# Moving four products per sequence from VectorE to ScalarE, and zero products on TensorE, in a Mamba and mixture-of-experts layer

## What is computed

```python
dA = jnp.exp(dt[..., None] * A)                      # 512 channels, 16 states
dBu = (dt * xc)[..., None] * Bm[:, :, None, :]
_, h = jax.lax.associative_scan(comb, (dA, dBu), axis=1)
y = jnp.einsum('blds,bls->bld', h, Cm) + D_skip * xc
y = y * jax.nn.silu(z)
return x + y @ W_out
```

## Time and profile before

| | |
|---|---|
| three runs, median (lowest to highest) | 1532.35 us (1527.24 to 1533.11) |
| profiled execution, its own time | 1532.31 us |
| span of its instructions | 1529.8 us |
| mean granted clock of TensorE, share of full | 0.934 |
| busy: PE, PEld, DVE, ACT, POOL | 1316.2, 1065.5, 1224.3, 786.7, 1044.4 us |

### The profile page before, as it was taken

The page is one execution under the profiler, slowest core; times in us unless marked ns, Lnnn a source line. Parts: engine busy times, 40 slices in busy tenths (PEclk is TensorE's granted clock), DMA queues, the critical chain, the costliest instruction groups (busy, mean ns, idle before and its releaser), DMA issues.

```text
span 1529.8 us, 26003 instructions
## 1 busy us (share of the span) xinstructions
PE 1316.2 (86%) x8004; PEld 1065.5 (70%) x8004; DVE 1224.3 (80%) x2149; ACT 786.7 (51%) x1385; POOL 1044.4 (68%) x943
## 2 busy tenths in 40 slices
PE   8567786877877998898798799979999999999997
PEld 3345564565555766666666566768899999999997
DVE  5889999999989999999999998988465555555554
ACT  4766767767866885886887687667000000000000
POOL 2775888799989899989999988987433352222222
PEclk9778898889979999999999999999999999999999
DMA  7212121324224344244343233577967797766662
GB/s 224 97 56 63 55 56 49 97 73 88 81 71 138 115 139 124 75 142 146 106 129 122 76 115 106 183 238 219 303 191 204 217 275 203 210 196 190 200 205 76
DMA packets 129344, 216.34 MB, mean 141 GB/s; under 512 B 17948, under 2 KB 74792, under 8 KB 129080
## 3 DMA queue, kind: packets, MB, share of 16 engines
q1 hardware_dynamic: 110376, 183.86, 39.1%
q0 software_dynamic: 16064, 27.62, 7.1%
q10 hardware_dynamic: 2768, 3.21, 0.9%
HBM read 178.34 MB, written 37.22 MB: 141 GB/s over the span
## 4 chain that ended last, share of the span: by engine, by line
PE 45%; POOL 18%; DVE 16%; issue 11%; ACT 7%; DMA 2%; SPq 1%; POOLq 0%; DVEq 0%; ACTq 0%
PE psum L1719 14%; PE psum L1735 13%; POOL dBu L885 12%; DVE w_sb L2022 8%; PE psum L1526 6%; DVE y L2033 3%; PE psum L1535 2%; ACT psum L1140 2%; ACT hc L1124 2%; PE psum L1687 1%; POOL rows_d L803 1%; PE psum L1674 1%; DVE w_sb L2003 1%; PE psum L1492 1%; DVE xc L2003 1%
## 5 line engine op out<-in xcount | busy, mean ns | idle before, releaser
L885 POOL TENSOR_TENSOR dBu<-w_sb,brep 128x512 f32<-128x512 f32 x512 | 642.9, 1319 | 35.5 <-issue 14.8
L2022 DVE TENSOR_TENSOR_SCAN w_sb<-psum,dBu 128x512 f32<-128x512 f32 x512 | 611.7, 1212 | 54.3 <-ACT psum L1140 34.3
L1140 ACT ACTIVATE psum<-w_sb,aneg 128x512 f32<-128x512 f32 x512 | 350.2, 692 | 123.0 <-DVE w_sb L2022 120.1
L1526 PE MATMUL psum<-ident,w_sb 128*128 128x128 f32 x2048 | 306.2, 297 | 116.8 <-DVE y L2033 73.8
L1526 PEld LDWEIGHTS psum<-ident,w_sb 128*128 128x128 f32 x2048 | 250.1, 152 | 195.1 <-DVE y L2033 108.3
L872 POOL DMA_INDIRECT out<-dBu,token x59 | 92.2, 1563 | 296.3 <-DMA out<-dBu,token 231.8
L1124 ACT ACTIVATE hc<-psum,ct 128x512 f32<-128x512 f32 x256 | 175.0, 683 | 106.1 <-PE psum L1526 73.8
L1535 PE MATMUL psum<-ident,hc 128*128 128x128 f32 x1024 | 168.2, 295 | 35.3 <-ACT hc L1124 24.4
L1535 PEld LDWEIGHTS psum<-ident,hc 128*128 128x128 f32 x1024 | 130.3, 151 | 76.8 <-ACT hc L1124 38.4
L2033 DVE SCALAR_TENSOR_TENSOR y<-psum,ct,y 128x512 f32<-128x512 f32 x240 | 174.9, 729 | 10.7 <-PE psum L1526 9.7
L1719 PE MATMUL psum<-xn,win 128*128 128x128 f32 x928 | 110.1, 278 | 3.2 <-issue 3.2
(11 more groups left out here) (274 smaller groups left out, 1747.8 us busy)
## 6 DMA issues: line engine op xcount, KB each, us to landing
brep<-b_d SPq DMA_DIRECT2D x128, 256.0 KB, 4.0
expert_pieces<-in_W SPq DMA_DIRECT2D x30, 1024.0 KB, 5.9
win<-in_W SPq DMA_DIRECT2D x29, 1024.0 KB
expert_pieces<-in_W SPq DMA_DIRECT2D x42, 512.0 KB, 5.3
dBu<-rows_d SPq DMA_DIRECT2D x35, 257.0 KB, 2.9
w_sb<-in_W SPq DMA_DIRECT2D x8, 1024.0 KB, 10.1
xg<-rows_d SPq DMA_DIRECT2D x22, 257.0 KB, 2.8
h_d<-hmod SPq DMA_DIRECT2D x8, 512.0 KB, 4.0
```

Of the source, the lines that this page charges most:

```text
L885: nc.gpsimd.tensor_tensor(dBu[:, i % RING, :], u[p][:, c, :], brep[:, s % 4, :], ALU.mult).then_inc(s_dBu, 1)
L1140: nc.scalar.activation(dA[:, i % DA_RING, :], dt[p][:, c, :], ACT.Exp, scale=aneg[:, c, s:s + 1]).then_inc(s_dA, 1)
L1526: last = nc.tensor.transpose(T[:, i // DT, c * P:(c + 1) * P], hs[s % 2][:, c, i * P:(i + 1) * P], ident[:, :])
L2022: nc.vector.tensor_tensor_scan(hs[s % 2][:, c, :], dA[:, i % DA_RING, :], dBu[:, (n * UNITS + i) % RING, :], 0.0, ALU.mult, ALU.add).then_ ...
```

## The change

The two products of state 0 move from VectorE to ScalarE in all eight sequences (`times_c_begin`; it writes `y` itself, so VectorE's form for state 0 goes). In sequences 0 to 6 the second-tile products of states 3 and 5 also move to ScalarE (`times_c_apart`), each into a tile of its own; `y_t` adds these to tile 1 with eight more transposes. TensorE multiplies zeros three times ahead of sequence 0's states, and three times after `xf_t` in state 9 of sequences 1 to 3. In sequence 7, `out_proj` leaves out the identity products, and VectorE adds the residual (`hres`) instead, one addition per half.

```diff
+APART = (3, 5)
...
+        def states_apart(n):
+            return APART if n < NB - 1 else ()
...
+            def times_c_begin(n, p, k):
+                if k == 0:
+                    act.wait_ge(s_c, n + 1)
+                    after(act, s_base, n - 1)
+                act.wait_ge(s_tr, n * UNITS + 2 * k + 1)
+                nc.scalar.activation(y[p][:, k, :], T[:, 0, :], ACT.Copy, scale=ct[:, p, k, 0:1]).then_inc(s_y, 1)
+
+            def times_c_apart(n, p, s):
+                act.wait_ge(s_tr, n * UNITS + TI * s + 3)
+                if s == APART[0]:
+                    after(act, s_yT, n)
...
+                nc.scalar.activation(apart(s), T[:, 0, :], ACT.Copy, scale=ct[:, p, 1, s:s + 1]).then_inc(s_y, 1)
...
+                    if s == 1:
+                        times_c_begin(n, p, 0)
                     times_c_before(n, p, s, 0, has_o)
                     if has_p and s == 1:
                         norm(n + 1, (0, 1))
...
                     decays(n, p, s, (2,), has_o)
+                    if s == 1:
+                        times_c_begin(n, p, 1)
...
+                    if s - 1 in states_apart(n):
+                        times_c_apart(n, p, s - 1)
                     decays(n, p, s, (3,), has_o)
...
                 for i in range(DT):
-                    for c in range(CH):
-                        last = nc.tensor.transpose(YT[:, i, c * P:(c + 1) * P], y[n % 2][:, i, c * P:(c + 1) * P], ident[:, :])
+                    parts = [y[n % 2][:, i, :]] + [apart(s) for s in states_apart(n) if i == 1]
...
                 at = slice((i % 2) * D, (i % 2 + 1) * D)
-                nc.tensor.matmul(Q[:, OB, at], ident[:, :], hres[:, i, :], start=True, stop=False)
+                if n < NB - 1:
+                    nc.tensor.matmul(Q[:, OB, at], ident[:, :], hres[:, i, :], start=True, stop=False)
...
+                if not has_o:
+                    pe.wait_ge(s_sp0, 2)
+                    pe.wait_ge(s_relu0, CH)
+                    for i in range(3):
+                        nc.tensor.matmul(T[:, 1, :], zeros[:, :], ones[:, :].unsqueeze(1).to_broadcast([P, TI, P]), start=True, stop=True)
                 for s in range(NS):
...
                         xf_t(n - 1)
+                        if n <= 3:
+                            add_zeros(3)
...
+                if n == NB - 1:
+                    dve.wait_ge(s_hload, 16 * NB)
+                    link(nc.vector.tensor_tensor(projected, hres[:, at, :], projected, ALU.add), n)
...
-                    add_y(n, p, s, 0)
+                    if s > 0:
+                        add_y(n, p, s, 0)
...
-                    add_y(n, p, s, 1)
+                    if s > 0 and s not in states_apart(n):
+                        add_y(n, p, s, 1)
```

More of the change, by code:

```diff
@@ L133, in program @@
         hc = sb("hc", [P, 2, DIN])
+        apart_first = sb("second_tile_apart", [P, 2, DIN])
         gT = sb("gT", [P, CH, L])
@@ L338, in program, with apart @@
         BANK = (1, 0, 1, 0)
+        def states_apart(n):
+            return APART if n < NB - 1 else ()
+        def apart(s):
+            j = APART.index(s)
+            if j < 2:
+                return apart_first[:, j, :]
+            return modo[:, 2 * j - 4:2 * j - 2, :].rearrange("p m d -> p (m d)")
         XB, OB = 0, 1
@@ L1124, in times_c @@
                 nc.scalar.activation(hc[:, k, :], T[:, 1, :], ACT.Copy, scale=ct[:, p, DT + k, s:s + 1]).then_inc(s_hc, 1)
+            def times_c_begin(n, p, k):
[8 more added lines that the diff above has]
+                    after(act, s_yT, n)
+                if s > 12:
+                    after(act, s_base, n)
+                nc.scalar.activation(apart(s), T[:, 0, :], ACT.Copy, scale=ct[:, p, 1, s:s + 1]).then_inc(s_y, 1)
             def times_c_before(n, p, s, k, has_before):
@@ L1548, in y_t @@
                 for i in range(DT):
-                    for c in range(CH):
-                        last = nc.tensor.transpose(YT[:, i, c * P:(c + 1) * P], y[n % 2][:, i, c * P:(c + 1) * P], ident[:, :])
+                    parts = [y[n % 2][:, i, :]] + [apart(s) for s in states_apart(n) if i == 1]
+                    for j, part in enumerate(parts):
+                        for c in range(CH):
+                            last = nc.tensor.matmul(YT[:, i, c * P:(c + 1) * P], part[:, c * P:(c + 1) * P], ident[:, :],
+                                                    start=(j == 0 and c == 0), stop=(j == len(parts) - 1), is_transpose=True,
+                                                    skip_group_check=True)
                 last.then_inc(s_yT, 1)
@@ L1555, in out_proj @@
                     after(pe, s_xnt, projected)
-                    pe.wait_ge(s_hload, 16 * (n + 1))
+                    if n < NB - 1:
+                        pe.wait_ge(s_hload, 16 * (n + 1))
                 if i == 2:
@@ L1563, in out_proj @@
                         pe.wait_ge(s_gate, n * CH + c + 1)
-                    last = nc.tensor.matmul(Q[:, OB, at], gT[:, c, i * P:(i + 1) * P], wout[:, c, :], start=False, stop=(c == CH - 1))
+                    last = nc.tensor.matmul(Q[:, OB, at], gT[:, c, i * P:(i + 1) * P], wout[:, c, :],
+                                            start=(n == NB - 1 and c == 0), stop=(c == CH - 1))
                 last.then_inc(s_op, 1)
@@ L2027, in add_y @@
                 c_s = ct[:, p, i, s:s + 1]
-                if s == 0:
-                    after(dve, s_base, n - 1)
-                    ins = nc.vector.tensor_scalar(y[p][:, i, :], T[:, 0, :], c_s, None, ALU.mult)
-                else:
-                    dve.wait_ge(s_y, DT * (n * NS + s - 1) + i + 1)
-                    ins = nc.vector.scalar_tensor_tensor(y[p][:, i, :], T[:, 0, :], c_s, y[p][:, i, :], ALU.mult, ALU.add)
-                ins.then_inc(s_y, 1)
+                dve.wait_ge(s_y, DT * (n * NS + s - 1) + i + 1)
+                nc.vector.scalar_tensor_tensor(y[p][:, i, :], T[:, 0, :], c_s, y[p][:, i, :], ALU.mult, ALU.add).then_inc(s_y, 1)
             def o_skip(n, p):
```

## The result

The changed kernel takes 1541.29 us (median of 11 runs, 1538.81 to 1554.24), the kernel before 1531.83 in as many: a ratio of 1.0069, interval 1.0051 to 1.0087. It is slower by more than the 0.5% that a measurement can tell. The forecast was 1531.0. The profiled execution took 1540.64 us, with a span of 1538.8.

The account below looks back on a forecast made before the run. VectorE was taken as nearly full in the recurrence, with ScalarE's room varying by state, and TensorE as the epilogue's bound. 4.75 - 8.3 + 3.8 - 1.7 = -1.45 us from 1532.31 gave 1530.9, rounded to 1531; range 1514 to 1541.

Parts of the forecast that it names:

- the zeros of state 9: TensorE's three zero products in sequences 1 to 3: 3.8 us lost in sum, bounds 3.2 won and 9 lost.
- the 8.3 us of states 3 and 5: Second-tile products moved to ScalarE: 13 x 0.64 = 8.3 us won, as ScalarE's idle time fits them.
- 1.0 won in sequence 1: Zeros just ahead of 10.2 us at clock 0.50: up to 3.2 us back if lifted, less 1.8 own cost.
- the working: The prediction's own sum over the changed places, apart from its rivals: -1.45 us, so 1531 us.
- 9 lost: The losing bound on the zeros' term, against 3.2 us won at the other end.
- The walk: States 3 and 5: ScalarE's product fits before its next decay, the fourth scan still finds it; 0.64 us won each.
- State 0, 4.75 us lost: Products moved to ScalarE, which has no room: later fourth decay, extra y transposes; 0.2 + 0.6 + 1.95 + 2.0 us lost.
- The projection, 1.7 us won: Epilogue: four identity products of 0.43 us leave a TensorE that never pauses; VectorE's additions hide in idle time.
- The first: Rival: VectorE bounds everywhere, all 30 products give 0.64 us each, zeros hidden; 1511.4 us, chance 0.20.
- The third: Rival: zeros keep TensorE at 2.4 GHz through sequence 1's stage and cost nothing; 1523.9 us, chance 0.10.
- The second, the other side: Rival: dt projection after state 9; zeros cost fully, late tiles halve states 3 and 5's win; 1539.3 to 1543, chance 0.13.
- late tiles: The second rival's reason for losing half of states 3 and 5's win, leaving 4.15 us won.

## Why the prediction was wrong

Two steps of the sum failed: the zeros of state 9, whose term left out the low clock behind them, and the 8.3 us of states 3 and 5. In the profiled executions, after less before, the 9.0 us of the span come from these places (the roundings add 0.1):

| place | forecast | measured |
|---|---|---|
| states 0 to 3, all sequences | +4.75 | +2.7 |
| states 4 to 7, all sequences | -8.3 | -5.0, of which -4.2 in sequences 1 to 6 |
| states 10 to 15, sequences 1 to 3 | +3.8 | +10.0 |
| behind the last scan | -1.7 | -2.6 |
| ahead of the first scan; states 8 and 9; states 10 to 15 elsewhere | nothing | +0.4, +2.4, +1.2 |

**The zeros of state 9, 3.8 us lost**, as 1.8 and 3.0 lost in sequences 3 and 2 and 1.0 won in sequence 1. The own cost was sized well: 2.9 + 2.5 + 1.5 = 6.9 us in sequences 1 to 3, for the 1.8, 3.0 and 1.8 of the working. What failed was the clock beside it. I counted the clock as a gain in sequence 1 only, with "no gain" as the other end. In the trace of the change two more low stretches stand there than before, 2.4 us each behind dt, and the one in sequence 1 stayed, 6.8 us long for 10.2; that gave back 1.3 us where up to 3.2 were hoped for. 6.9 + 2 x 2.4 - 1.3 = 10.4 us is what state 10 to 13 grew by in the three sequences. The bound of "9 lost" had no such term. In the times, leaving the zeros out is worth 6.4 us. That the zeros themselves bring the stretches is not shown: with six of them one remained, sequences without any have them in other kernels, and no run put other work of the same length in their place.

**States 3 and 5, 8.3 us won.** By the times this is the larger miss. Without the zeros the sum gives 1527.2 us, and that kernel took 1534.89; states 3 and 5 alone took 1537.06, with a ratio of 1.0037 to the kernel before. The walk was right for each state (0.6 us in states 4 and 6) and stopped too early. "Where a stall goes, what is late next" was not asked for state 7, where a fixed block of ScalarE gives back 0.5 of state 5's 0.6 us. In the rows that leaves 0.7 us a sequence, 4.2 in six. Why the times do not show even this is open. In the profiled execution of states 3 and 5 alone, the low stretches of sequences 4 and 5 cost 6.8 us and the stretch behind the last scan 8.3, more than the 4.2; whether the moved states bring them is not shown.

**State 0, 4.75 us lost.** The waits came where they were walked. In sequences 1 and 2 their cost did not: VectorE's freed time covered them. In sequences 4 to 6 it came together with the eight transposes of the tiles kept apart: states 0 to 3 took 0.9 to 1.2 us more in the changed kernel, for 0.65 forecast, part of it from a stretch at the lower clock that moved from state 2 to state 3. With state 0 alone, and so without these transposes, the same states kept their length. In the rows the term is 2.7 us in the changed kernel and near nothing for state 0 alone; as a time, alone, the ratio gives 4.4 us, with an interval from 0.5 to 8.6.

**The projection, 1.7 us won**: 1.84 alone; 2.6 in the changed kernel's stretch behind the last scan.

**The rivals.** The first (VectorE the bound, 1511) fell: VectorE's busy time fell as it says, and nothing else did. The third (zeros hold the clock) fell on the same rows as the working's gain in sequence 1. The Trainium skill, "TensorE: Matmul & The Clock Gate", section "What's actually happening", takes activity to be what releases the clock; here TensorE was busy through the zeros and the stage behind them, and the granted clock fell to 0.50 in it. The second, the other side, gave 1539.3 to 1543, and the time was 1541.29. Its place was right, and half of what states 3 and 5 were to win was lost, though to the block in state 7 and not to late tiles. Its price was near: a set cost 6.9 / 3 = 2.3 us of its own, under the 2.7 from which it was to decide, and 10.4 / 3 = 3.5 with the clock. That the total fell into its range is in part luck, since a low clock behind the zeros was no term of it, and what states 8 to 15 added elsewhere was none either. It had 0.13, too little, since the working itself had the two ways to lose and no more than a guess to win.

## What to carry to other kernels

Work taken from a nearly full engine is worth what the next state waits for, so follow each win until the engine that you gave the work to has had its next long block. Do not put work on the path of TensorE to buy clock: price it at its full duration less the idle time in front of it, and price the clock from both sides. In a kernel whose stages repeat with a steady length, a low-clock stretch can stand in a place where the others wait for TensorE in several repeats at once, or in none; a gain of 1 to 4 us from such an edit has to be read from the rows of its stage, over one that is free of low stretches, and not from the total alone.

## What the runs showed that I had not expected

Low stretches can be reproducible. In the one profiled execution with only the epilogue changed, those in sequences 1 to 7 fell in the same places as before, and each state's scans took the same time within 0.1 us. And they recur: with state 3's product alone they begin at 650.2, 779.9 and 909.6 us in sequences 4 to 6, 129.7 apart where these sequences last 130.1 and 130.0 us. A stretch that recurs with the sequences costs its 3.5 us or so in each of them. What sets the place is not shown, and with one trace for each kernel, whose executions lie up to 22 us apart, it is not shown that all of them have the stretches alike.

A better mean clock need not be a better time. The changed kernel has 0.941 against 0.934 in the profiled executions and is slower, since the gain lies in sequence 0, where TensorE is hardly waited for. Over the executions of one kernel, though, clock and time go together: of the kernel before, two at 0.927 and 0.940 took 1542.57 and 1527.4 us. It is no strict rule: one at 0.934 took 1542.52.
